# A graph network's relational convolutions: three bf16 pieces become two float32r halves, and nine dense chunks take the place of seven

## The reference

```python
def rgcn_conv(x, src, dst, etype, W, root, bias):
    seg = dst * R + etype
    agg = segment_sum(x[src], seg, n * R)
    cnt = segment_sum(ones, seg, n * R)
    agg = where(cnt > 0, agg / maximum(cnt, 1), 0).reshape(n, R, -1)
    return einsum('nrd,rdk->nk', agg, W) + x @ root + bias

h = concatenate([x, node_emb[node_type]])            # 128 + 128 features
h = relu(rgcn_conv(h, ..., W1, root1, b1))           # to 256 features
h = relu(rgcn_conv(h, ..., W2, root2, b2))           # to 128
h = relu(rgcn_conv(h, ..., W3, root3, b3))           # to 128
return layernorm(x + h)
```

## Time and profile before

| | us |
|---|---|
| median of 3 runs | 6051.39 (6045.1 to 6054.39) |
| profiled execution, its own time | 6035.35 |
| its span | 6033.5 |
| start of the first gather of the first convolution | 1314.7 |
| ... of the second | 3573.3 |
| ... of the third | 4797.5 |

### The profile page before, as it was taken

The page is one execution under the profiler, slowest core; times in us unless marked ns, Lnnn a source line. Parts: engine busy times, 40 slices in busy tenths (PEclk is TensorE's granted clock), DMA queues, the critical chain, the costliest instruction groups (busy, mean ns, idle before and its releaser), DMA issues. The chain is left out here.

```text
span 6033.5 us, 91554 instructions
## 1 busy us (share of the span) xinstructions
PE 4630.4 (77%) x34588; PEld 2926.8 (49%) x34588; DVE 2966.5 (49%) x7467; ACT 1296.2 (21%) x2385; POOL 3583.5 (59%) x3576
## 2 busy tenths in 40 slices
PE   2798999976666666666665558888888798999888
PEld 1466666643333333333333335555555455555555
DVE  6898861137788888787783221222212212222222
ACT  2566640013334343343341000000000000000000
POOL 5000000027777777777777747777777677777776
PEclk6799999987778878877886669999999899999999
DMA  3223226544444444454453335655656555555554
GB/s 90 111 107 138 107 107 230 218 167 134 130 138 140 131 141 138 129 146 134 122 149 110 114 129 158 198 189 176 195 158 197 184 161 169 165 163 166 169 158 124
DMA packets 428453, 903.90 MB, mean 150 GB/s; under 512 B 71170, under 2 KB 335116, under 8 KB 406124
## 3 DMA queue, kind: packets, MB, share of 16 engines
q0 software_dynamic: 169216, 348.44, 21.1%
q1 hardware_dynamic: 126580, 450.83, 20.6%
q10 hardware_dynamic: 132216, 98.74, 5.2%
HBM read 692.22 MB, written 205.05 MB: 149 GB/s over the span
## 5 line engine op out<-in xcount | busy, mean ns | idle before, releaser
L1402 POOL DMA_INDIRECT messages<-table,src_rows x2552 | 2584.3, 1013 | 853.7 <-issue 752.0
L1453 PE MATMUL couple_bank<-slices,pieces 128*128 128x384 fp8e4 x10290 | 1809.3, 333 | 0.0
L1453 PEld LDWEIGHTS couple_bank<-slices,pieces 128*128 128x128 bf16 x10290 | 1006.3, 100 | 653.1 <-issue 65.7
L1691 DVE TENSOR_TENSOR sums<-sums,bank 128x120 f32 x873 | 236.5, 271 | 1861.6 <-PE bank L1415 1799.4
L1415 PE MATMUL bank<-group_hot,messages 128*128 128x120 bf16 x10476 | 790.8, 233 | 460.4 <-DMA messages<-table,src_rows 302.4
L1402 POOL DMA_INDIRECT messages<-table,rel_rows x940 | 914.4, 973 | 342.4 <-issue 279.7
L1415 PEld LDWEIGHTS bank<-group_hot,messages 128*128 128x128 bf16 x10476 | 697.3, 107 | 677.6 <-issue 582.4
L1679 DVE TENSOR_SCALAR rel_hot<-couple_bank,rel_dense 128x490 bf16<-128x490 f32 x1344 | 952.5, 709 | 0.0
L1561 ACT CAST stage<-couple_bank 128x980 fp8e4<-128x980 f32 x672 | 656.1, 976 | 1110.4 <-PE couple_bank L1431 1109.2
L1431 PE MATMUL couple_bank<-rel_hot,lo_dense_hot 128*128 128x490 bf16 x1344 | 477.8, 444 | 457.5 <-ACT stage L1561 320.2
L1383 POOL IOTA iota_rel_i<- 128x250 int32 (+1 forms) x2 | 1.5, 776 | 1182.6 <-DMA table<-typed_rows 1182.6
(11 more groups left out here) (269 smaller groups left out, 3696.0 us busy)
## 6 DMA issues: line engine op xcount, KB each, us to landing
slices<-relations_d SPq DMA_DIRECT2D x70, 1200.0 KB, 5.7
slices<-relations_d SPq DMA_DIRECT2D x70, 1152.0 KB, 5.5
adjacency_d<-adjacency SPq DMA_DIRECT2D x15, 4704.0 KB, 14.5
adjacency<-adjacency_d SPq DMA_DIRECT2D x15, 4704.0 KB, 14.9
relations_d<-stage ACTq DMA_DIRECT2D x84, 500.0 KB
messages<-table,src_rows POOLq DMA_INDIRECT x2552
relations_d<-stage ACTq DMA_DIRECT2D x84, 480.0 KB
inverse<-inverse_d SPq DMA_DIRECT2D x52, 640.0 KB, 5.0
```

Of the source, the lines that this page charges most:

```text
L1402: pool.indirect_dma_start(messages[:, i % MESSAGES, t, 0:ROWS[v]], None, GATHERED[v], bass.IndirectOffsetOnAxis(ap=rows[:, e:e + 1], axis= ...
L1453: mm = pe.matmul(bank[DENSE_BANKS[K % 2]][:, 0:CHUNK], pieces[M % PIECE_RING][:, tile % PIECE_TILES, piece * P:(piece + 1) * P], slice_of_ ...
L1691: vec.tensor_tensor(sums[:, ds(base, GROUP_COLS)], sums[:, ds(base, GROUP_COLS)], from_bank[:, 0:GROUP_COLS], ALU.add).then_inc(sums_added, 1)
```

## The change

**Features** are held as two float32r halves, 256 four-byte words to a row (260 with the type in table 1, whose 4 type words now come first): ACT's copy into a float32r tile keeps the leading bits, DVE subtracts it once from the value and writes the rest. The middle piece, `rest_w` and the steps for them go; the second convolution's finish takes 7 halves in place of 9, the first's 9 in place of 12. Each group takes 8 matmuls in place of 12. The type matmuls take 128 weight columns in place of 3.

**Adjacency.** Both operands of a float32r matmul are four bytes wide, so `slices` stays fp8 and is expanded: a *lot* of 2 or 3 tiles is copied to one of three float32r buffers `lots`, by ACT for two of every three lots and by DVE for the third, as soon as PE has summed the lot three before. A slice is now 17 or 16 tiles, a task 18 lots and 98 matmuls.

**Share.** 9 chunks are dense in place of 7: the plans give 403, 185 and 185 groups, 0, 45 and 45 tasks; 864 couples are built in place of 672, spread over nearly all halves of the first convolution in place of one to a half.

**Buffers.** `MESSAGES` 6 to 3, `LEAD` 4 to 2, `pieces` 8 to 7 blocks. The first slices of the second convolution are loaded ahead of the first's last window in place of its third from last.

```diff
-MESSAGES = 6
-ROW = PIECES * FEAT
-TYPED_ROW = ROW + 4
+MESSAGES = 3
+HALVES = 2
+ROW = HALVES * FEAT
+TYPE_WORDS = 4
+TYPED_ROW = TYPE_WORDS + ROW
...
-CHUNKS_DENSE = 7
-DENSE_CHUNKS = (0, 7, 7)
+CHUNKS_DENSE = 9
+DENSE_CHUNKS = (0, 9, 9)
...
-SLICE_TILES = (25, 24)
+SLICE_TILES = (17, 16, 16)
...
-PIECE_RING = PIECE_BLOCKS + 1
-TASK_STEPS = NODE_TILES * PIECES
+PIECE_RING = PIECE_BLOCKS
+TASK_STEPS = NODE_TILES * HALVES
+SLICE_LOTS = 6
+TASK_LOTS = SLICES * SLICE_LOTS
+LOT_RING = 3
+LOT_TILES = 3
...
-            length = 12 if conv == 0 else 9
+            length = (9, 7, 9)[conv]
...
+        self.lot_at = [summed_at(self.lot_tiles(u - LOT_RING)) + 1 if u >= LOT_RING else 0 for u in range(self.lots)]
...
-            ("messages", [P, MESSAGES, GROUP, TYPED_ROW], bf16), ("group_hot", [P, MESSAGES, GROUP, GROUP_COLS], bf16), ...
+            ("messages", [P, MESSAGES, GROUP, TYPED_ROW], f32r), ("group_hot", [P, MESSAGES, GROUP, GROUP_COLS], f32r), ...
...
-        LEAD = 4
+        LEAD = 2
...
-        couple_at = lambda half: half - 2 * (REL_TICK + 1)
+        BUILD_HALVES = PLANS[0].half_ticks - 2 * (REL_TICK + 1) - 4
+        couple_half = lambda j: 2 * (REL_TICK + 1) + j * BUILD_HALVES // COUPLES
...
+        def expand(engine, copy, v, u):
+
+            lot = TASKS_BEFORE[v] * TASK_LOTS + u
+            n, m = divmod(u % TASK_LOTS, SLICE_LOTS)
+            J = (TASKS_BEFORE[v] + u // TASK_LOTS) * SLICES + n
+            if m in (0, 2):
+                engine.wait_ge(slice_in[J % 2], 16 * (J // 2 + 1))
+            if u >= LOT_RING:
+                engine.wait_ge(dense_marks, marks_of(v, PLANS[v].lot_tiles(u - LOT_RING)))
+            elif v == 2:
+                engine.wait_ge(dense_marks, marks_of(v, 0))
...
+            return copy(to, of_slice[:, :, first:end, :])
...
                 for t in range(GROUP):
-                    for piece in range(PIECES):
-                        mm = pe.matmul(to[:, 0:GROUP_COLS], messages[:, i % MESSAGES, t, piece * P:(piece + 1) * P], group_hot[:, i % MESSAGES, t, :],
...
+                    for half in range(HALVES):
+                        cols = slice(features + half * P, features + (half + 1) * P)
+                        mm = pe.matmul(to[:, 0:GROUP_COLS], messages[:, i % MESSAGES, t, cols], group_hot[:, i % MESSAGES, t, :],
...
-                slice_of_chunk = slices[:, J % SLICE_RING, 0:SLICE_TILES[n] * CHUNK].rearrange("p (s h) -> p s h", s=CHUNK_STAGES)
+                if tile == LOT_FIRST[l] and piece == 0:
+                    pe.wait_ge(*lots_made(lot))
...
-                               slice_of_chunk[:, :, within * STAGE_NODES:(within + 1) * STAGE_NODES], start=(at == 0), stop=(at == TASK_STEPS - 1))
-                if within == SLICE_TILES[n] - 1 and piece == PIECES - 1:
+                               lots[lot % LOT_RING][:, tile - LOT_FIRST[l], :, :].rearrange("p s d -> p (s d)"), start=(at == 0), stop=(at == TASK_STEPS - 1))
+                if piece == HALVES - 1:
                     mm.then_inc(dense_marks, 1)
...
+                    for u in lots_at[v].get(half, []):
+                        if u % LOT_RING < 2:
+                            expand(act, act.copy, v, u).then_inc(lots_by_act, 1)
...
+                    for u in lots_at[v].get(half, []):
+                        if u % LOT_RING == 2:
+                            expand(vec, vec.tensor_copy, v, u).then_inc(lots_by_vec, 1)
```

More of the change, by code:

```diff
@@ L86 @@
 PIECE_BLOCKS = NODE_TILES // PIECE_TILES
-PIECE_RING = PIECE_BLOCKS + 1
-TASK_STEPS = NODE_TILES * PIECES
+PIECE_RING = PIECE_BLOCKS
[4 more added lines that the diff above has]
+LOT_TILES = 3
+LOT_END = [SLICE_FIRST[n] + SLICE_TILES[n] * (m + 1) // SLICE_LOTS for n in range(SLICES) for m in range(SLICE_LOTS)]
+LOT_FIRST = [0] + LOT_END[:-1]
+assert max(end - first for first, end in zip(LOT_FIRST, LOT_END)) == LOT_TILES and TASK_LOTS % LOT_RING == 0
 assert PIECE_BLOCKS * PIECE_TILES == sum(SLICE_TILES) == NODE_TILES and FIRST_DENSE_PAIR % P == 0
@@ L177, in resnorm_gnn @@
 def resnorm_gnn(nc, a, out):
-    f32, i32, bf16, f16, f8 = mybir.dt.float32, mybir.dt.int32, mybir.dt.bfloat16, mybir.dt.float16, mybir.dt.float8e4
+    f32, f32r, i32, bf16, f16, f8 = mybir.dt.float32, mybir.dt.float32r, mybir.dt.int32, mybir.dt.bfloat16, mybir.dt.float16, mybir.dt.float8e4
     ALU, ACT, AX = mybir.AluOpType, mybir.ActivationFunctionType, mybir.AxisListType
@@ new lines, in resnorm_gnn @@
+        PIECE_BYTES, LOT_BYTES = PIECE_TILES * ROW * 4, LOT_TILES * CHUNK * 4
+        piece_homes = [all_end + n * PIECE_BYTES for n in range(2)]
+        lot_homes = [0, 0, all_end + 2 * PIECE_BYTES]
+        SLICES_AT = max(types_end, lot_homes[2] + LOT_BYTES)
+        (slices,), slices_end = lay(SLICES_AT, ("slices", [P, SLICE_RING, SLICE_TILES[0] * CHUNK], f8))
+        piece_homes += [slices_end + n * PIECE_BYTES for n in range(PIECE_RING - 2)]
+        lot_homes[0:2] = [piece_homes[-1] + PIECE_BYTES + n * LOT_BYTES for n in range(2)]
@@ new lines, in resnorm_gnn @@
+        assert lot_homes[1] + LOT_BYTES <= HOT
+        pieces = [lay(o, (f"pieces{n}", [P, PIECE_TILES, ROW], f32r))[0][0] for n, o in enumerate(piece_homes)]
+        lots = [lay(o, (f"lots{n}", [P, LOT_TILES, CHUNK_STAGES, STAGE_NODES], f32r))[0][0] for n, o in enumerate(lot_homes)]
+        SRC_ROWS, CODE_ROWS = weights_end - 2 * -(-EDGE_TILES * 4 // 32) * 32, weights_end - -(-EDGE_TILES * 4 // 32) * 32
+        LATER_TILES = -(-GROUP * PLANS[1].groups * 4 // 32) * 32
+        (relation_acc, w3, w3_root), dense_end = lay(
+            X1, ("relation_acc", [P, CHUNKS_DENSE, CHUNK], f32), ("w3", [P, RELATIONS, FEAT], f32), ("w3_root", [P, FEAT], f32))
@@ L1336, in conv_sync @@
                 load_block(1, m)
-            for j in range(2, SLICE_RING):
-                load_slice(1, j)
             for w in range(2):
@@ L1543, in conv_tensor @@
                     if v == 0:
-                        if 0 <= couple_at(half) < COUPLES:
-                            build(couple_at(half))
+                        for j in couples_at.get(half, []):
+                            if j < COUPLES:
+                                build(j)
                     if v == 2 and half - 2 in plan.task_end:
```

245 lines of the change are left out of this document (110 added, 135 removed).

## The result

| | before | after |
|---|---|---|
| median, us | 6052.9 (4 runs, 6045.1 to 6058.7) | 6549.2 (4 runs, 6542.3 to 6553.3) |
| ratio, 95% interval | | 1.0824 [1.0811, 1.0838] |
| span of the profiled execution | 6033.5 | 6551.5 |
| first convolution | 2258.6 | 3122.1 (+863.5) |
| second convolution | 1224 | 1054 (-170) |

The change makes the kernel 8.2% slower; 5800 us was forecast. The second and third convolution gained, by three quarters of what the forecast gave them. The first lost over four times the 200 us that it was charged. With 3.6 us more in the stage ahead, 6033.5 + 863.5 - 170 - 179 + 3.6 is the new span.

What follows compares the result with a forecast made beforehand. POOL's issue was taken to bound the second and third convolution, with three engines close in the first. 6035 + 200 - 460 + 10 = 5785 us, the median 16 us above, so 5800 us; range 5690 to 6340 us.

Steps and rivals of the forecast that it cites:

- the 200 us that it was charged: First convolution: +8 us a window, within +2 and +15, over 25 windows, +200 us.
- 1.07 batches a tick for 1, +0.23 us: First convolution, DVE: 432 batches for 336 spread over 403 ticks, adding 0.23 us a tick.
- D: Expansions for dense matmuls or the first convolution cost more than charged: 6040 us, or 5980 at +15 us a window; chance 0.10.
- About nothing at the lower: First convolution, PE: 12 float32r for 16 bf16 matmuls add 0.5 us a tick at upper clock, about nothing at lower.
- rival A: Group matmuls: below a certain width float32r is no faster than float32, 0.21 us for 120 columns; 6320 us, chance 0.25.
- The price of a float32r matmul at the upper clock: Group matmuls of 120 columns on PE: 0.11 us each, half a float32 matmul, with ends 0.0525 and 0.21.
- The dense matmul: Second and third convolution, PE: 0.163 us for 384 columns in one pass, 23.8 a tick, 3.89 us.
- Rival C: Dense matmuls dearer: load and columns in sequence, 0.27 us, 6740 us; two passes, 0.32, some 7200; chance 0.13.
- Lots: Second and third convolution: ACT and DVE expansions fit; 0.2 us a tick charged for waits and level engines.
- `group_hot`: First convolution, DVE: one-hots in four bytes take 0.65 us for 0.395, +0.26 us.
- The ring: First convolution: three groups for six let POOL run through less of a window; up to 10 us a window, mostly hidden before.
- The transfers: Second and third convolution: DMA traffic rises to some 250 GB/s, share near 0.8, still hidden with a thinner cover.

## Why the prediction was wrong, step by step

**"1.07 batches a tick for 1, +0.23 us"** is the step that failed. I counted how many batches a tick has and what they last, and not where in the half they stand. The row sequence of DVE shows a batch in a slot where PE waits for it little (0.75 us in the mean, when at all); I carried that over, although the change gives the batches new halves and leaves the code that runs them behind `add`. In its place the runs showed a wait: PE's second couple of a tick stands 3.0 us behind the chain of group, addition and four pairs. This was worth 420 us of the 863 on the first way of the account and 296 on the other, and no rival named it: D put the first convolution at +15 us a window, which would be +375 us, from work and not from order.

**"About nothing at the lower"** clock for the group matmuls in the first convolution was the second. I compared 0.11 us, a price made from rows at the upper clock, with the bf16 price at the lower. The price doubles with the clock here: 12 matmuls take 2.79 us at the lower, against 2221.36 - 2219.53 = 1.83 us for the 16 in bf16 (first tick of the earlier trace rows; the couple behind them is the row below), +1.0 us a tick. And the lower clock held for 84% of the stretch, not 38%: the forecast had kept the clock of before. So the 0.22 to 0.24 us measured at the lower clock lie near rival A's 0.21 us, and the 403 us that float32r costs on one way (278 on the other) near its +425. That is a coincidence and no proof of A, which had this price at the upper clock, from moving columns and passes: there it is 0.105 to 0.128 us, and the run with 4 weight columns shows that the load makes it.

```profile
2221.36 1.00 PE L1431 MATMUL couple_bank<-rel_hot,lo_dense_hot 128*128 128x490 bf16 x2
```

**The price of a float32r matmul at the upper clock** was right: 0.11 us was taken. PE's timeline in the third convolution, whose group and dense matmuls are those of the second (answers to the earlier trace rows):

```profile
5801.77 2.09 PE L1497 MATMUL couple_bank<-lots,pieces 128*128 128x384 f32 x11
5803.70 1.00 PE L1462 MATMUL bank<-group_hot,messages 128*128 128x120 f32 x8
5804.54 0.86 PE L1511 MATMUL bank<-dense_scaled,w 128*128 128x384 f32 x2
...
5807.75 4.57 PE L1497 MATMUL couple_bank<-lots,pieces 128*128 128x384 f32 x24
5812.15 1.00 PE L1462 MATMUL bank<-group_hot,messages 128*128 128x120 f32 x8
```

Eight take 5804.54 - 5803.70 = 0.84 us, 0.105 each; in the first convolution eight at the upper clock take 2248.88 - 2247.86 = 1.02 us, 0.128 each. The Trainium skill, "TensorE: Matmul & The Clock Gate", section "LDWEIGHTS", gave an estimate of 0.107 us; the trace agrees at the upper clock and not at the lower, where the price is twice that, and the run with 4 weight columns shows that the load is the reason.

**The dense matmul** is the term that was too small in these two convolutions. It was taken at 0.163 us; 11 take 1.93 us and 24 take 4.40 us, 0.175 and 0.183 each. At 23.8 a tick that is +0.3 to +0.5 us, and the tick is 5.52 us where 5.25 was forecast: 0.27 us x 370 ticks = 100 us, against the 111 us by which both convolutions missed their gain. What makes it dearer was not tested; the weight loads of these matmuls are busy for 685 of the 900 us, where those of the bf16 ones were for 379 of the same time, so the load is a candidate. Rival C fell: at 0.183 us against its 0.27 and 0.32, load and columns do overlap.

**Lots** were charged 0.2 us a tick with waits for a DVE expansion of 1.35 us. It took 0.76 us in the median (row below), PE's matmuls waited 17 us for lots in the whole run, and D's mechanism for the second and third convolution fell. The 0.2 us itself was near: PE is idle for (900 - 862) / 163 = 0.23 us a tick, 21 of the 38 us for gathered rows and 10 for lots.

```profile
L1285 DVE CAST lots<-slices x540: 727/761/1012, 4436.5 to 6530.0; 128x1152 fp32r<-128x1152 fp8e4 x180
```

**`group_hot`** in four bytes was forecast at 0.65 us and takes 0.64. The Trainium skill, "VectorE: DVE Perf Modes", section "What auto-detection actually checks", had led to the same 0.25 us more, and the trace now agrees: 0.64 us for 0.388 to 0.395 with 16-bit values.

**The ring** was charged up to 10 us a window, mostly hidden, within +200 us for all. In the kernel before it costs 134 us by itself and 147 with the couples spread and the batch ahead, 5.4 to 5.9 us a window, which fits. The transfers stayed hidden, at a share of 0.76 with 251 GB/s for the 0.8 and 250 of the forecast.

So the gain came as forecast, its size 24% off: fewer ticks, each a little longer and now bound by PE. That bf16 pieces would not have had it with 9 chunks is an estimate, as no run tried them: 45 x 147 / 185 = 35.8 dense matmuls a tick at 0.163 us, 0.63 us for the group and 0.25 for finishing give 6.7 us, and 185 x 6.7 = 1240 us against the 1224 of before. The loss came from an order that the forecast had not read (296 to 420 us) and from float32r in the first convolution, whose price at the lower clock it had put at nothing (278 to 403 us).

## What to carry to other kernels

When a change gives an operation new places, by a table or by a fraction, look for every place that it can now fall on and ask at each what its engine waits for just ahead of it, and who needs its result how soon behind it: a wait in front of the batch then costs as if it were part of the batch. When busy times fall on all engines while the tick grows, look for a chain through two engines instead of an engine that is full. And price a new type of matmul by its weight load and at both clocks, per stage: here float32r cost where 120 moving columns do not cover the load, and came with a gain where 384 nearly do.

## What the runs showed of the hardware

- A float32r matmul of 120 columns lasts 0.105 to 0.128 us at 2.4 GHz and 0.215 to 0.24 us at 1.2 GHz with 128 weight columns, and 0.057 and 0.10 us with 4. It follows the load, and the load follows TensorE's clock: one load of the type matmuls is 0.19 us long at its shortest and 0.33 in the median of the first convolution. In bf16 it is 1.28 / 12 = 0.107 us at the lower clock.
- DVE expands 1152 fp8 values to float32r in 0.76 us, 0.66 ns a value, where its two-source float32 operations take 1.04 ns.
- The granted clock of the stretch from 1500 to 3000 us was 0.81 before, 0.75 with the couples spread and the batch ahead, 0.71 with the batch behind, and 0.73 with the ring of 3 and nothing else, all in bf16 with nearly the same work on PE (925 to 999 us busy); 0.58 after, 0.62 with the batch ahead, 0.66 and 0.69 with bf16 views, and 0.75 with real bf16 pieces. So neither float32r nor PE's waits alone set it. **What lowers it stays open**: no run held the waits and the matmuls' types fixed and moved only the clock, and every step above, the 278 and 403 us of float32r and the 420 us of the order too, holds what it costs through the clock as well as by itself.
